# Two gated cross-attention layers on Trainium2: head scores as four 128-row matmuls per pair, in place of six 64-row matmuls

## The reference

```python
# layer 0, attention: 16 heads of 64
xn = _layernorm(x, ln_gamma, ln_beta)
q = (xn @ w_q).reshape(B, SQ, NUM_HEADS, DIM_HEAD)
kv = context @ w_kv                      # context: 16 x 375 x 256
k, v = jnp.split(kv, 2, axis=-1)
scores = jnp.einsum('bqhd,bkhd->bhqk', q * SCALE, k)
attn = jax.nn.softmax(scores, axis=-1)
out = jnp.einsum('bhqk,bkhd->bqhd', attn, v).reshape(B, SQ, INNER)
out = out @ w_out + b_out
return out * jnp.tanh(gate[0])
# then: x + FFT-mixing layer; x + one-head attention over the same context;
# x + mixture of 16 experts, the best 4 of each row, weighted by a softmax
```

## Time and profile before

| | us |
|---|---|
| median of 3 runs | 1162.66 |
| lowest, highest | 1161.47, 1164.37 |
| the profiled execution | 1161.57 |
| its span, first to last instruction | 1159.8 |
| TensorE busy | 1075.9 (93%) |
| VectorE busy | 773.1 (67%) |
| ScalarE busy | 631.4 (54%) |
| GpSimd busy | 519.8 (45%) |

### The profile page before, as it was taken

The page is one execution under the profiler, slowest core; times in us unless marked ns, Lnnn a source line. Parts: engine busy times, 40 slices in busy tenths (PEclk is TensorE's granted clock), DMA queues, the critical chain, the costliest instruction groups (busy, mean ns, idle before and its releaser), DMA issues.

```text
span 1159.8 us, 22342 instructions
## 1 busy us (share of the span) xinstructions
PE 1075.9 (93%) x7361; PEld 930.8 (80%) x7361; DVE 773.1 (67%) x1963; ACT 631.4 (54%) x1676; POOL 519.8 (45%) x745
## 2 busy tenths in 40 slices
PE   3889999999999999999999999999999779899995
PEld 3688888888888888888788888888887668789983
DVE  2544677767676767776676777676766665686665
ACT  2533556555656565655556565656564545555650
POOL 3512345453535454454535354536354404565441
PEclk9989999999999999999999999999999888999998
DMA  5395882010101011010001010101000522234469
GB/s 150 96 329 207 309 297 63 5 34 9 30 27 31 27 31 35 23 35 22 23 16 32 8 38 9 31 9 31 5 18 9 176 83 78 99 108 152 133 198 287
DMA packets 82382, 95.82 MB, mean 83 GB/s; under 512 B 9291, under 2 KB 74445, under 8 KB 82272
## 3 DMA queue, kind: packets, MB, share of 16 engines
q1 hardware_dynamic: 41904, 44.94, 13.5%
q10 hardware_dynamic: 31520, 32.51, 7.9%
q0 software_dynamic: 8848, 16.96, 4.2%
HBM read 41.98 MB, written 52.39 MB: 81 GB/s over the span
## 4 chain that ended last, share of the span: by engine, by line
PE 61%; DVE 16%; ACT 10%; issue 6%; DMA 4%; POOL 3%; SPq 1%; DVEq 0%; ACTq 0%; POOLq 0%
PE ps_kv L1568 14%; PE ps_ot L1854 8%; PE ps_ot L1668 5%; PE ps_kv L1650 5%; PE ps_s L1811 5%; PE ps_pt L1821 5%; ACT prob L938 4%; DVE negmax L1467 3%; PE ps_pt L1780 3%; PE ps_ot L1793 3%; DVE pT_lo L1478 2%; DVE k_lo L1152 2%; ACT v_hi L928 2%; DMA zb<-places 2%; PE ps_ot L1712 2%
## 5 line engine op out<-in xcount | busy, mean ns | idle before, releaser
L855 POOL TENSOR_TENSOR prob<-prob,rinv 112x750 f32<-112x750 f32 x128 | 185.4, 1448 | 310.7 <-DVE rinv L1472 310.4
L938 ACT ACTIVATE prob<-ps_s,negmax 112x375 f32<-112x375 f32 x256 | 144.7, 570 | 236.4 <-DVE negmax L1467 236.4
L1478 DVE TENSOR_TENSOR pT_lo<-ps_pt,pT_hi 125x672 fp32r<-125x672 f32 x128 | 109.7, 857 | 77.0 <-ACT pT_hi L1051 77.0
L1568 PE MATMUL ps_kv<-ctxT_hi,wkv 128*128 128x376 f32 x512 | 141.6, 357 | 7.8 <-DVE v_lo L1156 3.8
L1467 DVE TENSOR_REDUCE negmax<-ps_s 112x2 f32<-112x750 f32 x128 | 119.0, 930 | 0.1
L1156 DVE TENSOR_TENSOR v_lo<-ps_kv,v_hi 125x512 fp32r<-125x512 f32 x96 | 66.4, 692 | 77.2 <-ACT v_hi L928 77.2
L1568 PE MATMUL ps_kv<-wkv,ctxT_hi 128*125 128x512 f32 x384 | 112.2, 414 | 3.6 <-DVE n_e L1116 2.3
L1821 PE MATMUL ps_pt<-ident,prob 112*125 112x112 f32 x768 | 104.9, 273 | 1.3 <-POOL prob L855 1.3
L814 POOL DMA_INDIRECT places<-ysb,place_i x72 | 70.3, 976 | 69.1 <-ACT ysb L1010 55.9
L1051 ACT ACTIVATE pT_hi<-ps_pt 125x672 fp32r<-125x672 f32 x128 | 93.5, 730 | 9.0 <-PE ps_pt L1821 1.0
L1821 PEld LDWEIGHTS ps_pt<-ident,prob 112*125 112x125 f32 x768 | 95.1, 191 | 1.7 <-POOL prob L855 1.7
(11 more groups left out here) (298 smaller groups left out, 2623.8 us busy)
## 6 DMA issues: line engine op xcount, KB each, us to landing
rows_by_expert<-stage_w ACTq DMA_DIRECT2D x16, 1920.0 KB, 7.3
xg<-rows_by_expert SPq DMA_DIRECT2D x72, 128.0 KB, 2.1
zb<-places SPq DMA_DIRECT2D x16, 448.0 KB, 15.0
arena<-in_L_ffn_mlp_w SPq DMA_DIRECT2D x24, 256.0 KB, 4.4
ctx_in<-in_ctx SPq DMA_DIRECT2D x16, 375.0 KB
acc<-in_L_xattn_w_kv SPq DMA_DIRECT2D x4, 512.0 KB, 13.1
stage_w<-in_L_ffn_mlp_w SPq DMA_DIRECT2D x8, 256.0 KB, 3.0
x_in<-in_x SPq DMA_DIRECT2D x16, 112.0 KB, 2.1
```

Of the source, the lines that this page charges most:

```text
L855: e_prob.done(eng.tensor_tensor(prob[0:TQ, p % 2, :, :], prob[0:TQ, p % 2, :, :], rinv[:, 2 * p:2 * p + 2].unsqueeze(2).broadcast_to([TQ, ...
L938: e_exp.done(eng.activation(prob[0:TQ, p % 2, half, :], S[0:TQ, half, 0:SK], ACT.Exp, bias=negmax[:, h:h + 1], accum_out=rowsum[:, h:h + 1]))
L1478: e_pt_lo.done(eng.tensor_tensor(pT_lo[:, :, :, :].rearrange("p h k t -> p h (k t)"), PT[0:KEYT, :, 0:NKEY * TQ], pT_hi[:, :, :, :].bitcas ...
L1568: last = eng.matmul(out_, lhs(i, k), rhs(j, k), start=(n == 1), stop=(n == KT * len(PASSES)))
```

## The change

The score group of a pair has four matmuls with 128 rows, two for each head. For head h, `kx[:, p, h]` holds the high part of its keys on partitions 0 to 63 and the low part of the same keys on 64 to 127. `qx_hi` holds the high part of the head's queries twice, on both halves; `qx_lo` holds the low part on the lower half and zeros on the upper. One matmul with `qx_hi` then gives high with high and high with low, one with `qx_lo` gives low with high.

The data come there in this way. ScalarE copies a key projection to `kx[:, p, 0]` (128 partitions) and then head 1's half once more, from partitions 64 to 127 of PSUM to 0 to 63 of `kx[:, p, 1]`. VectorE writes the low part to a small buffer `k_low`, and SyncE moves it with 2 DMAs of 64 x 376 numbers to the upper halves. The high and low parts of half the queries go to `q_nat`, and SyncE moves them with 6 DMAs of 64 x 448 numbers. That is 28 DMAs and 2.9 MB a batch. TensorE's scores wait for these DMAs (`f_q`, `f_k`) where they waited for VectorE.

SyncE's list is now written slot by slot, so that the moves stand between its loads. The projections have other slots: k2 and v2 one slot later, `x`, `c` and k0, k1 one slot earlier, q0 two earlier. The order of the others is kept. The buffer `acc` is gone: set-up matrices lie in `stage_w` and the zeros in a buffer of their own, and the order of the experts (`TURN`) is another.

```diff
-        k_hi = t("k_hi", [128, NP, SKE], F32R)
-        k_lo = t("k_lo", [128, NP, SKE], F32R)
-        q_hi = t("q_hi", [128, NP, TQ], F32R)
-        q_lo = t("q_lo", [128, NP, TQ], F32R)
+        kx = t("kx", [128, NP, 2, SKE], F32R)
+        qx_hi = t("qx_hi", [128, 2, NP, TQ], F32R)
...
-        KV_AT = (("k", 2, 0), ("v", 2, 1), ("k", 3, 3), ("q", 1, 4), ("k", 4, 5), ("v", 3, 6),
-                 ("k", 5, 7), ("v", 4, 8), ("k", 6, 9), ("v", 5, 10), ("k", 7, 11), ("x", 0, -6),
-                 ("c", 0, -4), ("c", 1, -3), ("q", 0, -2), ("k", 0, -2), ("k", 1, -1), ("v", 0, -1),
+        KV_AT = (("k", 2, 1), ("v", 2, 2), ("k", 3, 3), ("q", 1, 4), ("k", 4, 5), ("v", 3, 6),
+                 ("k", 5, 7), ("v", 4, 8), ("k", 6, 9), ("v", 5, 10), ("k", 7, 11), ("x", 0, -7),
+                 ("c", 0, -5), ("c", 1, -4), ("q", 0, -4), ("k", 0, -3), ("k", 1, -2), ("v", 0, -1),
                  ("v", 1, 0), ("r", 0, 36), ("e", 0, 38))
...
+            def move(step, kind, n):
+                eng.wait_ge(kv_dve, KV_LO[use_of(step, kind, n) + 1])
+                if kind == "q":
+                    pairs = slice(n * NP // 2, (n + 1) * NP // 2)
+                    for head in range(2):
+                        own = slice(64 * head, 64 * head + 64)
+                        for half in range(2):
+                            eng.dma_start(qx_hi[64 * half:64 * half + 64, head, pairs, :].bitcast(F32),
+                                          q_nat[own, 0, :, :].bitcast(F32)).then_inc(f_q, 16)
+                        eng.dma_start(qx_lo[0:64, head, pairs, :].bitcast(F32),
+                                      q_nat[own, 1, :, :].bitcast(F32)).then_inc(f_q, 16)
+                if kind == "k":
+                    for head in range(2):
+                        eng.dma_start(kx[64:128, n, head, :].bitcast(F32),
+                                      k_low[64 * head:64 * head + 64, n % 2, :].bitcast(F32)
+                                      ).then_inc(f_k[n % 2], 16)
+            for g in range(FIRST, LAST_BODY + 13):
+                for step, kind, n in kv_groups(g - 1):
+                    if kind in "qk":
+                        move(step, kind, n)
...
+                if g == 4:
+                    for n in range(4):
+                        eng.wait_ge(s_wkv_lo[n], 1)
+                    load(stage[:, ST_WK:ST_WK + KT, :], wide(Wk1), ld_stage)
...
                 if kind == "k":
-                    ins = eng.activation(k_hi[:, n, :], bank[:, 0:SKE], ACT.Copy)
+                    eng.activation(kx[:, n, 0, :], bank[:, 0:SKE], ACT.Copy)
+                    ins = eng.activation(kx[0:64, n, 1, :], bank[64:128, 0:SKE], ACT.Copy)
...
-                        eng.wait_ge(kv_dve, KV_LO[max(use_of(st, "q", p // 4), use_of(st, "k", p)) + 1])
+                        eng.wait_ge(f_q, queries(st.off, p // 4) + Q_MOVES)
+                        eng.wait_ge(f_k[p % 2], keys(st.off, p) + K_MOVES)
                         e_exp.wait_ge(eng, st, 2 * p)
-                        for n, (i, j) in enumerate(PASSES):
-                            for half in range(2):
-                                rows_ = slice(64 * half, 64 * half + 64)
-                                last = eng.matmul(S[0:TQ, half, 0:SKE], qq[i][rows_, p, :],
-                                                  kk[j][rows_, p, :], start=(n == 0),
-                                                  stop=(n == len(PASSES) - 1))
+                        for half in range(2):
+                            for n in range(2):
+                                last = eng.matmul(S[0:TQ, half, 0:SKE], qx[n][:, half, p, :], kx[:, p, half, :],
+                                                  start=(n == 0), stop=(n == 1))
```

More of the change, by code:

```diff
@@ L431, in program @@
         e_xn = event("e_xn", 1)
+        f_q, f_k = sem("f_q"), [sem(f"f_k{n}") for n in range(2)]
         e_s = event("e_s", NP)
@@ L464, in program @@
         ctxT = (ctxT_hi, ctxT_lo)
-        kk = (k_hi, k_lo)
-        qq = (q_hi, q_lo)
+        qx = (qx_hi, qx_lo)
         qk = (qk_hi, qk_lo)
@@ L513, in program, with queries, keys @@
             KV_LO.append(KV_LO[-1] + int(kind != "x"))
+        Q_MOVES, K_MOVES = 6 * 16, 2 * 16
+        def queries(b, half):
+            return Q_MOVES * (2 * b + half)
+        def keys(b, p):
+            return K_MOVES * ((NP * b + p) // 2)
         def use_of(step, kind, n):
@@ L613, in _ @@
                 load(b1_in[m], mlp1_b[:, m * 256:(m + 1) * 256], ld_stage)
-            e_xn.wait_ge(eng, BATCH[0], 1)
-            load_x(1)
-            for n in range(4):
-                eng.wait_ge(s_wkv_lo[n], 1)
-            load(stage[:, ST_WK:ST_WK + KT, :], wide(Wk1), ld_stage)
-            load(stage[:, ST_A:ST_A + KT, :], wide(Wq1), ld_stage)
-            load(stage[:, ST_RE:ST_RE + KT, :], wide(w_re), ld_stage)
-            load(stage[:, ST_IM:ST_IM + KT, :], wide(w_im), ld_stage)
@@ L622, in _ @@
-            for n, at in enumerate((ST_COS, ST_SIN, ST_NSIN)):
-                load(stage[:, at:at + KT, :], wide(dft[n]), ld_stage)
-            load(wo[:, :, :], wide(w_out), ld_w)
-            load(wv1[:, :, :], wide(Wv1), ld_w)
-            load(b2[:, :], mlp2_b, ld_w)
-            eng.wait_ge(kv_pe, use_of(ZERO, "c", 0) + 1)
-            load_ctx(1)
-            eng.wait_ge(s_su, 4)
-            for n, part in enumerate((b1_hi, b1_lo)):
-                eng.dma_start(b1_row[n * NE:(n + 1) * NE, :], part.bitcast(F32)).then_inc(ld_b1, 16)
@@ L652, in _ @@
-                if 6 <= b < 10:
-                    load_expert(eng, b - 6)
-            store_base(B - 3)
+                nx = due(g, -23)
+                if nx and nx.off >= 2:
+                    e_xn.wait_ge(eng, BATCH[nx.off - 1], 1)
+                    e_xb0.wait_ge(eng, BATCH[nx.off - 2], 1)
+                    load_x(nx.off)
+                nx = due(g, -16)
+                if nx and nx.off >= 2:
+                    eng.wait_ge(kv_pe, use_of(BATCH[nx.off - 1], "c", 0) + 1)
+                    if nx.off >= 3:
+                        e_tl.wait_ge(eng, BATCH[nx.off - 3], 8)
+                    load_ctx(nx.off)
+                    if nx.off == 6:
+                        eng.wait_ge(f_filled, 16)
+                        eng.wait_ge(f_spare, 16)
+                        eng.wait_ge(f_zero, 16 * NE)
+                    if 6 <= nx.off < 10:
+                        load_expert(eng, nx.off - 6)
@@ L655, in _ @@
+                tb = due(g, 40)
+                if tb:
+                    store_base(tb.off)
             eng.wait_ge(kv_pe, max(use_of(BATCH[B - 1], "k", NP - 1), use_of(BATCH[B - 1], "v", 5)) + 1)
```

87 lines of the change are left out of this document (50 added, 37 removed).

## The result

The changed kernel takes 1232.69 us (median, 1230.14 to 1233.23) against 1162.64 before: ratio 1.0597, 95% interval 1.0577 to 1.0617. It is slower, as forecast, but by 70 us and not by 31, and outside my range (1165 to 1215).

What follows compares the result with a forecast made beforehand. Each 54.7 us batch was taken as 34 us bound by TensorE and 20.7 by a ScalarE/VectorE latency chain. 1161.6 - 17 (score groups) + 34 (transposes) + 13 (start) + 2 (fills) = 1193.6, forecast 1194 us, range 1165 to 1215.

Steps and rivals of the forecast that it cites:

- Moves among the fills: Batches 0 to 2: a move lands some 2 us late among the zero fills; +2 us, bounds 0 and 10.
- The queue at the start: Batch 0, pair 4: scores wait for moves queued behind SyncE's 3.1 MB of loads; +13 us, bounds 0 and 18.
- The xn transposes: Slot 10 to 9: ScalarE's `qk_hi` comes later, the v projection waits for k6's low part; +2.4 a batch, +34 us.
- The second copy: ScalarE's second key copy, slot 5: `k_lo` and all behind it come 0.4 us later a batch.
- The score groups: TensorE: four 128-row matmuls without change of rows save 0.2 us a group, over 86 groups -17 us.
- as much waiting of before goes: Slot 12: `c1` and `q0` wait some 0.5 us for low parts, offset by about as much earlier waiting that disappears.
- The moves in the steady part: Steady batches: key and query moves land in time, k6's with 1.9 us to spare; cost 0.
- moves late in every batch: Rival: moves take 4 us to land in place of 2.1; +18, 1212 us; chance 0.10.
- TensorE is the bound: Rival: ScalarE's and VectorE's stretch has slack, all 128 groups gain, -26; 1137 or 1150 us; chance 0.08.
- no wait at the start: Rival: the moves get past SyncE's loads in batch 0, without the +13; 1181 us; chance 0.12.
- packing lost: Rival: score groups take four passes in place of three, change of rows gives nothing back; +15, 1226 us; chance 0.08.
- Only 0.4 a batch: Rival: the latency stretch grows only by 0.4 us a batch, v projection not waiting; 1167 us; chance 0.17.

Runs made afterwards that it cites:

- small fills: The changed kernel with zero fills of 9 of every 15 row blocks, the rest left out: 1211.15 us, ratio 1.0416.

## Why the prediction was wrong, step by step

The sign and the mechanisms held; the size was off by 38 us. The 71.7 us at batch 15 are 4.0 in the ramp (forecast 0), 18.5 at pair 4 (13), some 20 among the fills (2) and 29 in steady batches (34 - 17 = 17). The fills make half of the miss, the steady batches a third.

- **Moves among the fills: +2, bounds 0 and 10; measured some 20.** This step failed. I sized it as one landing 2 us late. In the trace the median move took 6.7 us to land in place of 2.1 and 1.4 us to issue in place of 0.6. Six of the nineteen pairs between pair 4 of batch 0 and batch 3 waited for their key move, 19.3 us together, one of them 7.0, and the clock fell behind the waits. The growth over this stretch is 25.3 us, some 5 of them steady; small fills take away 23. The earlier trace rows had shown a DMA share of 0.99, so landings much later than 2 us were to be thought of, in every batch that has fills, and I took one.
- **The queue at the start: +13, bounds 0 and 18; measured 18.5** (pair 4 at +22.5, less the 4.0 of pair 3). The mechanism was right, but it gave the time only up to the landing of the loads. Behind that came SyncE's issues (0.5 to 2.8 us each, not 0.4), a landing of 7.1 us beside a fill, and the fall of the clock (my 0 to 3). My row for that fall was misread in part: the single-column matmuls end at 72.8, and other work runs from there to 78 at the low clock.
- **The ramp: not in the sum; measured 4.0.** The first scores come 3.6 us late and the loads 3.4. It is there without any move (3.8) and with the slots alone in the kernel before (2.9), but not with the early transposes of xn alone (-0.4). So here it is the price of the earlier slots of the contexts, queries and keys; with these put back and the moves kept, the first scores are still 2.1 late and wait 1.8 for a move.
- **The xn transposes, +2.4 a batch, +34.** Each of its waits was there, and k7 came 2.2 late. The 2.4 held the late copies too. By themselves the transposes are 0.77 (from after) or some 0.9 (from before, estimated), all slots 1.4 and the copy 0.9 (from before).
- **The second copy, +0.4 a batch:** the chain showed it, 0.49 of waiting ahead of `k_low`, but alone it costs 0.9 a batch and 12 us where I had 6.
- **The score groups, -17:** -14 when changed alone. Sized well for that case.
- **The steady batch.** I wrote "near 56.5", and it is 56.64. But the terms of the sum didn't give that: 54.7 + 2.4 - 1.0 is 56.1. From k7 to the end of the batch I let five groups win 1.0 us; only 0.3 of it came back (2.2 late at k7, 1.93 over the batch). The single edits say the same: copy, slots and groups would add to 0.9 + 1.4 - 0.8 = 1.5, and together they make 1.9. That "as much waiting of before goes" as `c1` and `q0` add, 0.5 a batch, was the likely failure; no run isolates it. Had I carried my own 56.5 into the sum, fourteen batches of +1.8 made +25 in place of +17. That 56.5 came so close to 56.64 was luck.
- **The moves in the steady part, 0:** right, 0.1 a batch. The rival "moves late in every batch" is refuted, as are "TensorE is the bound", "no wait at the start" and "packing lost". "Only 0.4 a batch" is refuted too.

The range failed because its upper end added the rival to the forecast but not the bounds of the costs to each other: 13 to 18 and 2 to 10 alone reach 1207, and the steady part by the period 1215; the collision lay beyond its own bound, and the ramp was in neither.

What stays open: what ScalarE's copy L962 waits for in the long batches of the kernel before on the slower chip (9.4 us in total in 300 to 900 us; the trace calls the releaser remote). And how the some 20 us of the collision divide between landing, issue and clock.

## What to carry to other kernels

A small transfer on the path costs what its queue and its neighbours make it cost: write down what is ahead of it in its own queue and which bulk transfers run at that time, and set the late landing against the cover of every move in that stretch, not of one. When a transfer is given an earlier slot to hide it, check which work was moved along that didn't need it; here queries and keys needed theirs (66 us more without, though xn's was put back too) and xn didn't (13 us less without). Before two runs of single edits are compared, look whether a wait that neither edit touches stands in one and not in the other: here one such wait made 1.2 us of a batch. Check the sum of the terms against the period that you expect.
